# Scatter-adds of a mixture-of-experts kernel: registers loaded ahead of the waits, and a second table entry for every fourth tile

## What is computed

```python
x = hidden_states.reshape(-1, H)                      # 2048 x 256, layer-normed
router_logits = x @ wg.T                              # 8 experts
probs = softmax(router_logits)
topk_w, topk_idx = top_k(probs, 2)
topk_w = topk_w / sum(topk_w)
...
h1 = einsum('th,eih->tei', x, w1)                     # I = 512
h3 = einsum('th,eih->tei', x, w3)
y = einsum('tei,ehi->teh', silu(h1) * h3, w2)
out = einsum('te,teh->th', expert_w, y)
x = x + out
```

## Time and profile before

| | |
|---|---|
| median of 3 runs | 527.78 us (525.57 to 528.47) |
| profiled execution | 526.67 us, of which the span on the core is 524.2 us |
| PE busy | 496.8 us, 95% |
| DVE / ACT / POOL busy | 378.8 / 286.7 / 278.0 us |
| mean granted PE clock | 0.989 |
| scatter-adds (L968) | 39, 62.9 us busy on POOL |
| gathers (L942) | 39, 40.4 us busy on POOL |
| small operations (L966) | 32 |

### The profile page before, as it was taken

The page is one execution under the profiler, slowest core; times in us unless marked ns, Lnnn a source line. Parts: engine busy times, 40 slices in busy tenths (PEclk is TensorE's granted clock), DMA queues, the critical chain, the costliest instruction groups (busy, mean ns, idle before and its releaser), DMA issues.

```text
span 524.2 us, 10993 instructions
## 1 busy us (share of the span) xinstructions
PE 496.8 (95%) x3686; PEld 326.6 (62%) x3686; DVE 378.8 (72%) x978; ACT 286.7 (55%) x575; POOL 278.0 (53%) x312
## 2 busy tenths in 40 slices
PE   7899999999999999999999999999999899999970
PEld 3576766656666676766667776656666566666650
DVE  5899887588967668877889899997878444444440
ACT  4556767647466745773749657664454344433320
POOL 4463203003642708994496763545754756757573
PEclk9999999999999999999999999999999999999995
DMA  8002533246877537985598770248597689778683
GB/s 273 19 25 77 171 102 108 94 96 105 149 175 121 148 74 168 156 147 167 98 191 178 158 264 20 90 111 114 110 194 110 113 131 122 137 117 139 102 93 38
DMA packets 135313, 65.60 MB, mean 125 GB/s; under 512 B 109757, under 2 KB 126590, under 8 KB 135262
## 3 DMA queue, kind: packets, MB, share of 16 engines
q1 hardware_dynamic: 127774, 54.69, 48.6%
q0 software_dynamic: 7488, 10.23, 12.2%
HBM read 28.19 MB, written 10.35 MB: 74 GB/s over the span
## 4 chain that ended last, share of the span: by engine, by line
PE 58%; DVE 11%; DMA 8%; issue 8%; ACT 6%; POOL 4%; POOLq 2%; SPq 1%; DVEq 0%; ACTq 0%
PE ps L1205 47%; DMA out<-y,qst 5%; DMA probT<-prob 3%; PE ps L1300 3%; PE ps L1302 3%; PE ps L1301 3%; ACT ps L1016 2%; DVE cmax L1744 2%; POOL out L968 2%; POOLq L962 1%; POOL y L942 1%; ACT tT L1002 1%; ACT prob L1015 1%; PE ps L1214 1%; PE ps L1261 1%
## 5 line engine op out<-in xcount | busy, mean ns | idle before, releaser
L1205 PE MATMUL ps<-arena,probT 128*128 128x256 f16 (+2 forms) x1092 | 180.0, 318 | 4.0 <-issue 1.8
L1205 PEld LDWEIGHTS ps<-arena,probT 128*128 128x128 f16 (+1 forms) x1092 | 104.4, 97 | 61.0 <-issue 8.3
L1205 PE MATMUL ps<-arena,qT 128*128 128x512 f16 (+1 forms) x384 | 69.1, 332 | 1.0 <-DVE prob L1885 0.7
L968 POOL DMA_INDIRECT out<-y,qst x39 | 62.9, 1612 | 13.1 <-issue 7.8
L1015 ACT ACTIVATE prob<-ps,nbias 128x512 f16<-128x512 f32 x64 | 39.0, 609 | 50.9 <-DVE nbias L1750 50.9
L1143 ACT ACTIVATE w1m<-ps 128x512 f32<-128x512 f32 x39 | 23.3, 598 | 74.7 <-PE ps L1205 56.6
L1205 PE MATMUL ps<-arena,tT 128*128 x468 | 57.4, 273 | 0.9 <-DVE tT L2445 0.6
L791 POOL TENSOR_TENSOR rstd<-veps,expo 128x1 f32<-128x1 f32 x16 | 9.0, 563 | 91.8 <-DVE veps L1779 91.8
L1205 PEld LDWEIGHTS ps<-arena,qT 128*128 128x128 f16 x384 | 32.5, 97 | 36.0 <-issue 1.7
L942 POOL DMA_INDIRECT y<-hrow,qst x39 | 40.4, 1037 | 24.1 <-DVE qst L2107 12.8
L1205 PE MATMUL ps<-tT 128*128 128x512 f16 (+3 forms) x234 | 48.8, 346 | 1.4 <-DVE probT L1810 0.8
(11 more groups left out here) (240 smaller groups left out, 919.5 us busy)
## 6 DMA issues: line engine op xcount, KB each, us to landing
stage<-we_in SPq DMA_DIRECT2D x33, 256.0 KB, 3.0
prob<-we_in SPq DMA_DIRECT2D x15, 256.0 KB, 3.8
xin<-x_in SPq DMA_DIRECT2D x16, 128.0 KB, 2.7
out<-y SPq DMA_DIRECT2D x16, 128.0 KB
hrow<-tT SPq DMA_DIRECT2D x4, 512.0 KB, 3.5
y<-x_in SPq DMA_DIRECT2D x3, 512.0 KB, 7.6
stage<-z_in SPq DMA_DIRECT2D x4, 256.0 KB, 5.7
prob<-w_in SPq DMA_DIRECT2D x4, 256.0 KB, 3.2
```

Of the source, the lines that this page charges most:

```text
L968: g.indirect_dma_start(out[:rows_of(p), :], bass.IndirectOffsetOnAxis(ridx[:, n:n + 1], 0), ys[:, n % RING, :], None, compute_op=ALU.add). ...
L1205: r = t.matmul(o, lhs(a), rhs(b), start=first and n == 0, stop=last and n == 2)
```

## The change

The table gets a second row, `before2[n]` = 16 * differ[n] + adds[n-2], in a free part of the buffer `u`; one more DVE operation for each phase writes it, next to the one that writes `before`. In add(n) the registers are loaded first, ahead of every wait on other adds (behind the wait for the table itself). For n % 4 == 1 from 9 on, where the tile isn't alone (13, 21, 25, 29, 33 and 37), a second register is loaded from `before2`, and the wait on the slot of n-2 uses it; the unconditional wait for add n-2 stays for the tiles that stand alone and for tile 5. The small operation now runs for every tile but 0, those that stand alone too. The wait for the rows (e_y) stays where it was, between the small operation and the DMA.

```diff
+        before2 = inside(u, 400, [P, NJ], U32)
...
             def add(n):
 
                 p = phase_of(n)
+                alone = n <= RING or n == PHASES[p][1]
+                if not alone:
+                    if n == PHASES[p][1] + 1 or n == RING + 1:
+                        wait(pool, "r_next", p + 1)
+                    done = pool.value_load(before[0:1, n:n + 1], min_val=16, max_val=16 * NJ)
+                    if n % RING == 1 and n > RING + 1:
+                        done2 = pool.value_load(before2[0:1, n:n + 1], min_val=16, max_val=16 * NJ)
                 wait(pool, "x1_out", 16 * TB * PHASES[p][0])
-                alone = n <= RING or n == PHASES[p][1]
                 if n > 2:
                     add_done(n - 3)
-                if n > 1 and (alone or n % RING == 1):
+                if n > 1 and (alone or n == RING + 1):
                     add_done(n - 2)
                 if n and alone:
                     add_done(n - 1)
                 if not alone:
-                    if n == PHASES[p][1] + 1 or n == RING + 1:
-                        wait(pool, "r_next", p + 1)
-                    done = pool.value_load(before[0:1, n:n + 1], min_val=16, max_val=16 * NJ)
                     pool.wait_ge(sm[f"e_add{(n - 1) % RING}"], done)
                     if n % RING != 1:
                         pool.wait_ge(sm[f"e_add{(n - 2) % RING}"], done)
+                    elif n > RING + 1:
+                        pool.wait_ge(sm[f"e_add{(n - 2) % RING}"], done2)
+                if n:
                     g.tensor_tensor(gap[:, n:n + 1], expo[:, 0:1], expo[:, 0:1], ALU.mult)
                 wait(pool, "e_y", n + 1)
...
                 link(v.tensor_tensor(differ[:, n0 + 1:n1], tabf[:, 0, n0 + 1:n1], tabf[:, 0, n0:n1 - 1], ALU.not_equal))
+                m0 = max(n0, 1)
+                v.scalar_tensor_tensor(before2[:, m0 + 1:n1], differ[:, m0 + 1:n1], 16.0, adds[:, m0 - 1:n1 - 2],
+                                       ALU.mult, ALU.add)
                 v.scalar_tensor_tensor(before[:, n0 + 1:n1], differ[:, n0 + 1:n1], 16.0, adds[:, n0:n1 - 1],
                                        ALU.mult, ALU.add).then_inc(sm["r_next"], 1)
```

## The result

The changed kernel takes **534.41 us** (median of 6 runs, 533.0 to 537.48), the kernel before 526.65 us (6 runs, 525.02 to 528.47): a ratio of 1.0152, 95% interval 1.0127 to 1.0176. It is slower by 8 us where 1.8 us of gain were forecast. Some 1.1 us of that profile's surplus are there at add 0 already (357.38 against 356.31). They aren't the change's: in the profile of the second set the same kernel has its add 0 at 356.10.

The account below looks back on a forecast made before the run. POOL's queue of scatter-adds, not PE, was taken to bound the kernel's end. Terms -1.54 (add 37), -0.43 (add 17), +0.10 (add 9), +0.10 (DVE) sum to -1.77: 527.78 to 526.0 us, range 523.3 to 528.7.

Parts of the forecast that it names:

- What bounds the kernel: End of kernel: POOL's queue of scatter-adds, not PE, sets the end; gains from add 9 on count whole, about 5 us at most.
- Add 37: In the tail, add 37 waits for 35; with the table's wait it would need only 34, so the last add comes 1.54 us earlier.
- Load ahead of the waits: 0 more: Register load in POOL's waiting adds: already hidden behind the wait for n-1, so moving it gains nothing beyond add 37's 1.54 us.
- Two of the signs that the prediction named for being wrong: Adds 17 to 33 stretched by more than they gained, and PE beginning to idle before 505.
- Small operation for adds that stand alone, -0.43 for add 17: Adds 1 to 4, 9, 17: a small operation before the DMA shortens landing to DMA; add 17 gains 0.43 us.
- The 0.84 in the prediction: Add 17 in the kernel before: time from the landing of add 16 (443.53) to add 17's issue (444.37), in us.
- Second load: POOL's sequencer: the extra register load could cost time only at add 29, and there 0; upper bound 0.2 us late.
- Add 9: Add 9 follows a gather; the added small operation lengthens start to start from 1.27 to 1.37 us, costing 0.10.
- Third DVE operation: DVE's extra table operation: free for phases 0 and 2, delays the phase 1 stretch near 378 by 0.10 us, ends 0 and 0.17.
- Landings fall otherwise: Rival, adds 9 to 38: one long landing becomes usual or one usual long, 2.2 us; 523.8 (chance 0.16) or 528.2 (0.13).
- The rival for slower: Scatter-add queue in HBM: adds 1.94 us apart, three in flight, make two chain landings long, costing 4.4 us; 530.4, chance 0.06.

Follow-up runs that it names:

- the second set: The changed kernel measured once more with no edit, beside another version on one chip: 534.01 us, ratio 1.0137.
- The slow kernels: The changed kernel (both measurements), the changed kernel without before2 and its load, and the kernel before with its x1_out wait moved onto the small operation: 533.86 to 534.45 us.
- the quick ones: The kernel before, 526.65 us, and five variants where the small operation or DMA carries the newest wait, ratios 0.9952 to 0.9978.
- the five with it parked: Changed kernel, n-1 wait first: not-alone adds; all; all, alone adds without small operation. Kernel before plus before2: alone; with n-1 wait on alone adds' DMA. Ratios 0.9952 to 0.9978.

## Why the prediction was wrong

**What bounds the kernel: right.** The adds on POOL set the end from add 9 on. The slow kernels took 114.4 to 117.8 us from add 9 to 38, the quick ones 105.2 to 107.9; where the chain grew past what the ring of four could take, PE was held too.

**Add 37: right to the hundredth.** 3.48 us to 1.94, -1.54. Adds 13, 21, 25, 29 and 33 gained nothing, as forecast.

**"Load ahead of the waits: 0 more": this step failed.** It compared when the load was done, and took it as given that the rest of the path, 0.07 us to the small operation and 0.34 to the add, stayed as it was. What the step moved was not only the load but a border: a load is an instruction that waits can hang on. With the load between them, x1_out and n-3 hung on the load, and n-1 was the first wait in front of the small operation. With the load gone from there all four stood before the small operation, and it got the oldest. Price: 0.46 to 0.50 us for each of 13 adds, 6.4 us, where I had written nothing. Shown from both sides, by moving one wait in each kernel (525.35 and 533.86). The profile of before held the hint. Add 37, whose landing wait was the sequencer's, had 0.64 us from small operation to add (513.38 to 514.02) where add 28 had 0.34. I counted the difference as part of the load. Two of the signs that the prediction named for being wrong came: adds 17 to 33 took 64.59 us instead of 60.34, and PE idled before 505.

What this rests on is also in the Trainium skill, "Perfetto Trace Analysis". Its section "Identifying Dependency Chains" says that further waits may be put into EventSemaphore instructions ahead of the instruction that has them. In its section "Per-instruction lifecycle: what the profiler-reported window actually captures" a GpSimd instruction is pushed into a wait queue with its wait, and the sequencer is then ready for the next. The traces here agree: the wait for n-1 has no row in the kernel before (L963) and 32 in the changed one (L967), and in the kernel before with x1_out moved such a row stands up to 4311 ns. The price of the one against the other, 0.50 us, is from the runs.

**Small operation for adds that stand alone, -0.43 for add 17: failed for the same reason.** It carried x1_out, and add 17 came 0.85 us behind the landing, as against 0.90 without it: -0.05. With the right wait the gain is there: 0.41 (0.26 on the DMA), 0.49 better than before. The 0.84 in the prediction came from a landing put 0.03 us ahead of the eviction of tile 20, where 0.09 is right.

**Second load: right.** Add 29 stands 1.99 us behind 28 before and after (500.44 to 502.43). **Add 9:** from the gather 1.35 us (408.31 to 409.66) instead of 1.27, +0.08 where 0.10 was put.

**Third DVE operation: right in size.** In the changed kernel the operation behind `before2` starts 0.08 us later (379.12 to 379.20). The list of phase 2 was ready 0.4 us later than before, reckoned from add 0; part of it stays unexplained.

**The rivals.** "Landings fall otherwise" was priced for one or two of them, 2.2 us each, and not as a shift of all. It happened beside the failed step. In the four profiles with the wait on the sequencer the fourteen landings average 4.47 to 4.76 us, in the before and the five with it parked 4.32 to 4.50. The groups touch, with one profile of each kernel. The difference of their means, 0.2 us, makes 3 us over fourteen and fills what 6.4 - 1.5 leaves of the 8 us. Its cause is open. It may be that PE, once held by the ring, and with it SP's transposes fall into step with the adds; no run tests this. The prediction had the adds share queues with SP's transposes. That isn't shown: the profile before has 10.23 MB on the software queue, which is what 39 gathers and 39 adds of 128 KB come to. The rival for slower had the place right, the queue of adds, and the wrong mechanism: the tail with adds 1.94 us apart landed as before. No rival had the program's waits as such in it. The range missed because I bounded the durations of instructions, and not what it costs when an instruction changes from waiting in the engine's queue to waiting in the sequencer.

## What to carry to other kernels

Where one engine's chain is made of waits, look at who carries the last one. Of the waits written ahead of an instruction the first stayed on it here, and the others stopped the sequencer: write the one that ends last first, and keep old ones behind it or on another instruction. Before moving an instruction out from between two waits, write down for every wait which instruction will carry it. In these profiles a wait without a row of its own was a carried one, or shared the row of its neighbour.

## What the runs showed of the hardware

Where a small POOL operation carries the wait that ends last, the sequencer is past the add behind it 0.03 us after the landing (495.74 for 495.71), and the add starts 0.34 us behind the operation. Where the sequencer does the waiting, it is past the add only 0.65 to 0.70 us after the landing, 0.43 to 0.48 us after the operation's start, and the add starts 0.65 to 0.69 us behind the operation. An indirect DMA that carries its own constant wait begins 0.26 us after the landing; with a small operation between that carries it, 0.41; with the wait on the sequencer, 0.82 to 0.91.
